# First mixture of a two-layer kernel: seven masked products of weight differences and one unmasked product per slot, router bias on TensorE, beta rows added during the scan, new orders

## The chip, the cores and the metric

The kernel runs on one core of a Trainium2 chip. The metric is the device time of one execution in microseconds, as the median of several runs. Engines are named as in the profile: PE is TensorE, DVE VectorE, ACT ScalarE, POOL GpSimd, SP SyncE, whose queue issues most DMAs.

## The reference, cut to what matters

Two layers over x of 16 x 512 tokens and 128 channels. Each has an attention-like half and a mixture of experts with adaLN modulation. The change touches the first layer: its state-space scan, and its mixture, in which each token goes through the one expert with the highest logit.

```python
h = _layernorm(x) * (1 + ca) + sa
x = x + ga * _L0_attn_ref(h, ...)       # scan over 512 tokens, then y = (y - mu) * rsqrt(var + eps) * gamma + beta
h = _layernorm(x) * (1 + cb) + sb
x = x + gb * _L0_ffn_ref(h, ...)

# _L0_ffn_ref, 8 experts:
logits = xt @ gate_w + gate_b
sel = jnp.argmax(softmax(logits), axis=-1)
onehot = one_hot(sel, 8)
y_all = einsum('td,edh->eth', xt, expert_w) + expert_b[:, None, :]
out = einsum('te,eth->th', onehot, y_all)
```

## The kernel before, in words

The program is a row of stages, each a block in which every engine has its own hand-written instruction list; the lists meet only through semaphores. A stage ends at a barrier of all engines (`end_phase`). Each engine runs its list strictly in order, so the order of the calls in a list is the schedule.

The tokens are cut into 16 slots `w` of 512 tokens (`C` = 4 tiles of 128). `x_tok` holds x with tokens on partitions, `xg` the scan's result.

**The scan** (block before `ssm.close()`). 16 groups of 8 channels pass through a pipeline, one step per group. PE multiplies the group into end states (L687), carries them over (L695) and writes outputs (L705 with `carry`, L709 with Toeplitz tiles `toep`). DVE masks (L646), adds (L652), reduces (L656) and spreads the end states into `carry` in three copies (L665), each a product of `ends` and a piece of `con`, both in SBUF. ACT stores the outputs (L634). SP loads twelve Toeplitz tiles (L623), each after the output product four groups before. POOL clears `carry` (L675) and then waits for the barrier.

**The first mixture** (block from `names = ("weights", ...`). For each slot:

- DVE: `statistics` (L1006, L1010) of the scan's result; `gamma` (L1034 for the first four slots, L1039 behind them); `joined` (L1049, L1053) adds to `x_tok`; `stats_x` and `shift_x_head` (L1017 to L1026) for the first four slots.
- POOL: `beta` (L883) adds the row ga * beta to `x_tok` before `joined`; `bias_pieces` (L888 to L899) cuts the experts' biases into three bf16 parts, with a one-time wait on six weight loads; the means and scales of the normalizations (L843 to L866).
- ACT: roots, normalizations, `feat` (L966), which writes the modulated and transposed features `f_t`; `hot_half` (L973); `scaled` (L979), which takes the finished product; squares (L924).
- PE: `turn` (L1124) transposes the normalized tiles, `logits` (L1132), `turn_hot` (L1140) transposes the one-hot choices, `bias` (L1156) starts the sum in PSUM, then eight products (L1160), one per expert, `ew0[:, e, :]` times `masked[e % 4]`, and `turn_back` (L1148).
- DVE: `best` (L1060 to L1072) adds the router's bias to the logits, takes the largest and the first that equals it, and writes the one-hot choices `hot`. `mask` (L1090), eight per slot, multiplies `f_t` by one expert's row of ones and zeros, spread over the partitions (`wide`). `added` (L1081) adds the product.
- SP: `load` (L800) fetches the rows ga * gamma and ga * beta of a slot; `kept` (L817) writes the choices to DRAM and `spread` (L822) reads them back broadcast to 128 partitions.

The eight masks share four buffers. So a mask waits for the product four before it, and a product for its mask:

```python
def mask(w, e):
    if e == 0:
        landed(dve, s_wide, w)
        done(dve, "feat", w)
    expert(dve, "product", w, e - 4)
    nc.vector.tensor_tensor(masked[e % 4][:, :], f_t[w % W][:, :], wide[w % W][:, e, :], ALU.mult)

def product(w, e):
    expert(pe, "masked", w, e)
    nc.tensor.matmul(ps[:, w % 2, :], ew0[:, e, :], masked[e % 4][:, :], start=False, stop=(e == E - 1))
```

`idle_products` (L69) are products of the identity that nobody reads; they stand where PE would wait.

## Time and profile before

| what | us |
|---|---|
| median of 3 runs (lowest, highest) | 947.99 (942.74, 949.33) |
| the profiled execution | 940.09 |
| its span, first to last instruction | 938.3 |
| PE, DVE, ACT, POOL busy in the span | 863.5, 773.4, 627.1, 566.3 |
| mean granted TensorE clock, share of full speed | 0.983 |
| scan, in us of the span | 98.5 to 142 |
| first mixture, in us of the span | 143.0 to 339.1 |

Busy times in rows of several instructions are of their union; a duration in the timeline runs from the first start to the last end. A matmul in fp32 stands as two records, and its end is modelled, so a product's pace is read from starts. Brackets behind an instruction give how long its engine had been idle and what ended that.

### The profile page before, as it was taken

The page shows a single profiled execution, that of the slowest core. Times are in us where ns is not written, and L with a number is a line of the kernel's source. Part 1 is how long each engine was busy: PE and PEld are TensorE (multiplying, and loading weights), DVE is VectorE, ACT ScalarE, POOL GpSimd, SP SyncE. Part 2 cuts the span into 40 slices and gives each one's busy share as a digit, 9 for nine tenths or more (in the row PEclk, how much of TensorE's full clock was granted, in tenths as well). Part 3 has the DMA queues.
Part 4 walks back from the last instruction along what each step waited for, and adds up shares of the span by engine and source line. Part 5 has one row for each costly group of instructions (what it writes and reads, how often), then busy time and mean ns, then how long its engine had stood idle before and what let it go on. Part 6 is the DMA issues. An engine that isn't in the chain of part 4 may idle for free.

```text
span 938.3 us, 24334 instructions
## 1 busy us (share of the span) xinstructions
PE 863.5 (92%) x7820; PEld 682.3 (73%) x7820; DVE 773.4 (82%) x2369; ACT 627.1 (67%) x1619; POOL 566.3 (60%) x551
## 2 busy tenths in 40 slices
PE   6979897898999979999999999999979999999990
PEld 5945677544454468888888888888758888888880
DVE  3988778999999736888999999999996866666996
ACT  3557123578788355567777777766567888888880
POOL 1211004397776215433888888888877777777773
PEclk9999998999999999999999999999999999999996
DMA  5330352333322212000011111111127765766987
GB/s 156 95 96 1 99 174 64 113 136 111 139 96 91 100 30 56 2 1 10 31 41 40 39 36 36 39 37 45 41 63 229 213 201 180 224 183 201 345 254 248
DMA packets 83465, 100.84 MB, mean 107 GB/s; under 512 B 15326, under 2 KB 65305, under 8 KB 81164
## 3 DMA queue, kind: packets, MB, share of 16 engines
q1 hardware_dynamic: 71388, 79.61, 27.7%
q0 software_dynamic: 8640, 17.97, 5.4%
q10 hardware_dynamic: 3312, 1.70, 0.6%
q8 instruction: 65, 1.06, 0.5%
q14 instruction: 60, 0.49, 0.2%
HBM read 75.71 MB, written 23.54 MB: 106 GB/s over the span
## 4 chain that ended last, share of the span: by engine, by line
PE 54%; DVE 3%; ACT 2%; issue 2%; DMA 1%; POOL 1%; SPq 0%; ACTq 0%; DVEq 0%; POOLq 0%
PE ps L2697 12%; PE ps L2435 12%; PE ps L2720 6%; PE ps L2451 4%; PE ps L2513 2%; PE ps L2426 2%; PE ps L2446 2%; PE ps L2680 2%; PE ps L2552 2%; PE ps L2568 2%; PE ps L2414 1%; PE ps L2401 1%; PE ps L2500 1%; POOL parts L1651 1%; PE ps L69 1%
## 5 line engine op out<-in xcount | busy, mean ns | idle before, releaser
L1618 POOL TENSOR_TENSOR kvb<-qk,v 128x1024 f32<-128x1024 f32 x64 | 127.1, 1990 | 71.7 <-DVE qk L1991 48.0
L1627 POOL DMA_INDIRECT rows_of<-payb,posu x128 | 143.8, 1124 | 39.5 <-issue 28.4
L2435 PE MATMUL ps<-con,kvb 128*128 128x128 f32 x1024 | 126.0, 276 | 0.0
L1160 PE MATMUL ps<-masked,ew 128*128 128x512 f32 x256 | 121.3, 603 | 2.3 <-DVE masked L1090 2.3
L2435 PEld LDWEIGHTS ps<-con,kvb 128*128 128x128 f32 x1024 | 119.4, 192 | 1.0 <-issue 1.0
L2362 DVE TENSOR_SCALAR qk<-ps,b 128x256 f32<-128x256 f32 x142 | 62.0, 478 | 46.8 <-PE ps L2697 41.6
L1651 POOL DMA_INDIRECT parts<-h,dest x72 | 79.6, 1106 | 23.6 <-issue 20.3
L1090 DVE TENSOR_TENSOR masked<-f_t,wide 128x512 f32<-128x512 f32 x128 | 86.9, 724 | 4.7 <-PE ps L1160 4.5
L1651 POOL DMA_INDIRECT parts<-gx,dest x70 | 77.8, 1111 | 21.4 <-issue 19.5
L1967 DVE TENSOR_TENSOR qc<-ps,qk 128x1024 f32<-128x1024 f32 x64 | 78.0, 1219 | 11.8 <-PE ps L2435 10.8
L1160 PEld LDWEIGHTS ps<-masked,ew 128*128 128x128 f32 x256 | 44.3, 190 | 43.9 <-issue 29.3
L2720 PE MATMUL ps<-w,f_t 128*128 x568 | 75.0, 275 | 0.0
L2720 PEld LDWEIGHTS ps<-w,f_t 128*128 128x128 f32 x568 | 69.0, 192 | 8.2
L1872 ACT ACTIVATE qk<-ps,b 128x256 f32<-128x256 f32 x142 | 59.6, 470 | 17.3 <-PE ps L2697 16.7
L2697 PE MATMUL ps<-qd,ex 128*128 128x256 f32 x288 | 68.1, 379 | 0.0
L2697 PE MATMUL ps<-qd,lg 128*128 128x256 f32 x280 | 66.3, 380 | 0.0
L69 PE MATMUL ps<-con 128*128 128x128 f32 x398 | 55.7, 294 | 4.9 <-PEq L74 3.9
L69 PEld LDWEIGHTS ps<-con 128*128 128x128 f32 x398 | 51.6, 207 | 8.1 <-issue 6.7
L2697 PEld LDWEIGHTS ps<-qd,ex 128*128 128x128 f32 x288 | 51.9, 190 | 5.6
L1877 ACT ACTIVATE nrm<-qk,limit 128x512 f32<-128x512 f32 x71 | 51.3, 722 | 6.8
L2251 DVE SCALAR_TENSOR_TENSOR f_t<-qk,nrm 128x512 f32<-128x512 f32 x71 | 49.2, 694 | 7.1 <-DVE qk L2362 0.8
L2697 PEld LDWEIGHTS ps<-qd,lg 128*128 128x128 f32 x280 | 50.5, 190 | 5.4
(375 smaller groups left out, 2142.4 us busy)
## 6 DMA issues: line engine op xcount, KB each, us to landing
wide<-hot_dram SPq DMA_DIRECT2D x16, 1024.0 KB, 4.6
kvb<-rows_of SPq DMA_DIRECT2D x71, 132.0 KB
ex<-in_w_dram SPq DMA_DIRECT2D x36, 256.0 KB
lg<-in_w_dram SPq DMA_DIRECT2D x35, 256.0 KB
toep<-taps_dram SPq DMA_DIRECT2D x16, 512.0 KB, 4.4
xg<-parts SPq DMA_DIRECT2D x16, 512.0 KB, 5.5
x_tok<-in_x_dram SPq DMA_DIRECT2D x16, 256.0 KB, 3.0
rows<-rows_dram SPq DMA_DIRECT2D x16, 192.0 KB, 3.1
```

What stands on the lines that cost most here:

```text
L69: nc.tensor.matmul(ps[:, bank, 0:P], k("ident"), k("ident"), start=True, stop=True)
L1090: nc.vector.tensor_tensor(masked[e % 4][:, :], f_t[w % W][:, :], wide[w % W][:, e, :], ALU.mult).then_inc(s["masked"], 1)
L1160: nc.tensor.matmul(ps[:, w % 2, :], ew0[:, e, :], masked[e % 4][:, :], start=False, stop=(e == E - 1)).then_inc(s["product"], 1)
L1618: nc.gpsimd.tensor_tensor(kv[g % KB][:, :, :].rearrange("p e (h d) -> p e h d", h=H), k_in, v_in, ALU.mult).then_inc(s["kv"], 1)
L1627: nc.gpsimd.indirect_dma_start(rows_of, bass.IndirectOffsetOnAxis(ap=posu[w % PR][:, slot, t:t + 1], axis=0), pay[w % PB][:, t, :], None). ...
L1651: nc.gpsimd.indirect_dma_start(parts, bass.IndirectOffsetOnAxis(ap=dest[:, at, c:c + 1], axis=0), yw[u][:, c, :], None).then_inc(s_out[u], 16)
L1872: last = nc.scalar.activation(glu[v % 2][:, f, :], ps[:, bank, f * SP:(f + 1) * SP], ACT.Relu, bias=b1[:, bass.ds(e * NF + f, 1)], scale=-1.0)
L1967: nc.vector.tensor_tensor(qc[g % 2][:, :, :], cum(g), q_in, ALU.mult).then_inc(s["qc"], 1)
L2362: last = nc.vector.tensor_scalar(lin[v % 2][:, f, :], ps[:, bank + 1, f * SP:(f + 1) * SP], b1[:, bass.ds(e * NF + 2 + f, 1)], 8.0, ALU.ad ...
L2435: last = nc.tensor.matmul(cum(g)[:, e, :], kv[g % KB][:, e, :], k("upto"), start=True, stop=True)
L2697: last = nc.tensor.matmul(ps[:, bank + f // 2, (f % 2) * SP:(f % 2 + 1) * SP], w1c[v % WC][:, f * P:(f + 1) * P], x_t[v % 2][:, :], start= ...
L2720: last = nc.tensor.matmul(to, act_t[v % 2][:, j, c * P:(c + 1) * P], w2[:, bass.ds(e * (2 * D) + j * D, D)], start=False, stop=(c == S - 1 ...
```

## The change

- The weights `ew0[e]` of experts 0 to 6 become differences to those of expert 7 (one POOL subtraction). A slot's sum is now an unmasked product of `f_t` with `ew0[7]` (`base`) and seven masked ones (`M` = 7); `base` starts the sum in PSUM, `bias` comes behind it. The four masked buffers go round over all masks, not per slot.
- The router's bias, divided by 8 and cut into three bf16 parts on 24 rows (`gb3`), is added on PE by a product with a tile of ones at the start of `logits`; `best` reads the logits from PSUM (two readers) and has no addition.
- The additions of the beta rows leave the mixture. SP loads all 16 rows, broadcast to 128 partitions (`betas`, 1 MB), and the weights at the start of the scan; POOL does the preparations and 16 additions to `x_tok` beside the scan. `rows` hold the gamma rows alone.
- The lists of POOL, ACT, DVE, SP and PE in the mixture have a new order; PE has fewer idle products.

```diff
+                    sp.dma_start(ebf[0:E, :], a["eb0"]).then_inc(s_ahead, 16)
+                    sp.dma_start(ebf[E:2 * E, :], a["eb0"]).then_inc(s_ahead, 16)
+                    sp.dma_start(ebf[2 * E:K3, :], a["eb0"]).then_inc(s_ahead, 16)
+                    sp.dma_start(gbf[:, :], a["gb0"].partition_broadcast(K3)).then_inc(s_ahead, 16)
+                    sp.dma_start(gw0[:, :], a["gw0"]).then_inc(s_ahead, 16)
+                    sp.dma_start(ew0[:, :, :], a["ew0"]).then_inc(s_ahead, 16)
+                    sp.dma_start(betas[:, :, :], rows_dram[:, D:2 * D].partition_broadcast(P)).then_inc(s_ahead, 16)
                     groups(sp, body)
...
                     for u in range(U):
                         nc.gpsimd.memset(carry[u][:, :, :], 0.0).then_inc(s_z, 1)
...
+                    pool.wait_ge(s_ahead, 7 * 16)
+                    pool.wait_ge(s_split, 3)
+                    nc.gpsimd.tensor_tensor(ew0[:, 0:M, :], ew0[:, 0:M, :], ew0[:, M:E, :].to_broadcast([P, M, D]), ALU.subtract).then_inc(s_ew, 1)
+                    pieces(s_split, ebf, ebh, ebr, 3, [which[:, j:j + 1] for j in range(2)])
...
+                    for b in range(B):
+                        at = x_tok[:, b * C:(b + 1) * C, :]
+                        nc.gpsimd.tensor_tensor(at, at, betas[:, b:b + 1, :].to_broadcast([P, C, D]), ALU.add).then_inc(s_beta, 1)
...
                         if e == 0:
                             landed(dve, s_wide, w)
                             done(dve, "feat", w)
-                        expert(dve, "product", w, e - 4)
-                        nc.vector.tensor_tensor(masked[e % 4][:, :], f_t[w % W][:, :], wide[w % W][:, e, :], ALU.mult).then_inc(s["masked"], 1)
...
+                        at = w * M + e
+                        if at >= 4:
+                            expert_product(dve, (at - 4) // M, (at - 4) % M)
+                        nc.vector.tensor_tensor(masked[at % 4][:, :], f_t[w % W][:, :], wide[w % W][:, e, :], ALU.mult).then_inc(s["masked"], 1)
...
-                            done(pe, "lg", w - 1)
+                            done(pe, "equal", w - 1)
+                            nc.tensor.matmul(ps[:, LOGIT, 0:C * E], one3[:, :], gb3[:, :, :].rearrange("p c e -> p (c e)"), start=True, stop=False)
                             done(pe, "feat", w)
...
+                    def base(w):
+                        done(pe, "moe_t", w - 2)
+                        done(pe, "feat", w)
+                        nc.tensor.matmul(ps[:, w % 2, :], ew0[:, M, :], f_t[w % W][:, :], start=True, stop=False).then_inc(s["plain"], 1)
...
-                    statistics(0); statistics(1); gamma(0); joined(0); stats_x(0); gamma(1); shift_x_head(0); joined(1); stats_x(1)
+                    statistics(0); gamma(0); joined(0); stats_x(0); statistics(1); shift_x_head(0); gamma(1); joined(1); stats_x(1)
```

On POOL, the mixture's list began like this before; L883 are the beta additions, L888 to L899 the bias pieces:

```order
L901 MEMSET eps 128x1
L902 TENSOR_SCALAR down<-con 128x8
L883 TENSOR_TENSOR x_tok<-x_tok,rows_73 128x512
L883 TENSOR_TENSOR x_tok<-x_tok,rows_74 128x512
L888 TENSOR_SCALAR which<-con 24x1 x2
L890 TENSOR_SCALAR which<-which 24x2
L893 CAST ebh<-ebf 24x128
L895 TENSOR_SCALAR ebr<-ebh,which 24x128
```

Now the scan's list of POOL ends like this, behind the subtraction of the experts' weights (L724) and the pieces of both biases; `betas` are the rows, L638 is the branch out of the scan's block:

```order
L711 CAST gbh<-gbf 24x8
L713 TENSOR_SCALAR gbr<-gbh,which 24x8
L715 TENSOR_TENSOR gbf<-gbf,gbr 24x8
L730 CAST gb_13<-gbf 24x32
L733 TENSOR_TENSOR x_tok<-x_tok,betas 128x512 x16
L638 UNCONDITIONAL_BRANCH
```

All sixteen additions moved in front of the barrier, and they stand in one run.

On DVE, the masks of slot 0 and the choice of slot 2 stood like this before:

```order
L1090 TENSOR_TENSOR masked_108<-f_t_92,wide_100 128x512
L1060 TENSOR_TENSOR logit<-ps,gb_72 128x32
L1063 TENSOR_REDUCE largest<-logit 128x4
L1065 TENSOR_TENSOR equal<-logit,largest 128x32
L1067 TENSOR_TENSOR equal<-equal,down 128x32
L1069 TENSOR_REDUCE lowest<-equal 128x4
L1072 TENSOR_TENSOR hot<-down,lowest 128x96
L1090 TENSOR_TENSOR masked_109<-f_t_92,wide_100 128x512
L1090 TENSOR_TENSOR masked_106<-f_t_93,wide_101 128x512
```

The same place now (`masked_114` is slot 0's last mask, `f_t_99` belongs to slot 1):

```order
L1106 TENSOR_TENSOR masked_114<-f_t_98,wide_106 128x512
L1043 SCALAR_TENSOR_TENSOR stat_89<-moments_x,stat_88 128x4
L1077 TENSOR_REDUCE largest<-ps 128x4
L1079 TENSOR_TENSOR equal<-ps,largest 128x32
L1081 TENSOR_TENSOR equal<-equal,down 128x32
L1083 TENSOR_REDUCE lowest<-equal 128x4
L1086 TENSOR_TENSOR hot<-down,lowest 128x96
L1106 TENSOR_TENSOR masked_115<-f_t_99,wide_107 128x512
```

The eighth mask and the addition to the logits are gone, and a shift of the head (L1043) stands behind the first masks.

On PE, the change from slot 6 to slot 7 before (L1132 logits of slot 9, L1156 the bias, L1140 the choices, L1148 the turn back):

```order
L1132 MATMUL ps<-gw_71,f_t_93 128x8 x4
L1156 MATMUL ps<-hot_b_99,ebx 128x512
L1160 MATMUL ps<-masked_106,ew_65 128x512
L1160 MATMUL ps<-masked_107,ew_65 128x512
L1140 MATMUL ps<-con,hot 24x128 x4
L1148 MATMUL ps<-con,moe_t_104 128x128 x4
```

and now, at the same slots (L1168 `base`, L1172 the bias, L1143 the ones times the router's bias, L1162 the turn back):

```order
L1176 MATMUL ps<-masked_112,ew_5 128x512
L1137 MATMUL ps<-con,xn_97 128x128 x4
L1168 MATMUL ps<-f_t_101,ew_5 128x512
L1172 MATMUL ps<-hot_b_105,ebx 128x512
L1143 MATMUL ps<-gb_13,one_14 128x32
L1146 MATMUL ps<-gw_18,f_t_99 128x8 x4
L1176 MATMUL ps<-masked_113,ew_5 128x512
L1162 MATMUL ps<-con,moe_t_110 128x128 x4
```

A product that waits for no mask stands at the slot's change, in the place of the eighth masked one.

## Rows read from the trace of the kernel before

**Rows 1.** Windows: stretch, then busy us (count) of PE, PEld, DVE, ACT, POOL.
```profile
98.50:142.00 43.50, 40.51 (x768) 28.09 (x768) 32.86 (x113) 9.55 (x16) 1.92 (x4) 1.00 0.51 147
...
143.00:173.40 30.40, 24.84 (x176) 22.70 (x176) 29.11 (x121) 13.30 (x34) 13.99 (x20) 0.89 0.31 96
173.40:309.50 136.10, 128.95 (x480) 64.97 (x480) 130.77 (x484) 106.65 (x331) 95.01 (x153) 1.00 0.31 111
309.50:331.70 22.20, 22.20 (x65) 10.06 (x64) 16.27 (x45) 6.91 (x27) 7.99 (x12) 1.00 0.23 86
```

**Rows 2.** Timeline of PE, one slot: start, us, engine, line, what.
```profile
236.88 0.66 PE L1148 MATMUL ps<-con,moe_t 128*128 128x128 f32 x4
...
239.53 3.60 PE L1160 MATMUL ps<-masked,ew 128*128 128x512 f32 x8
242.97 0.60 PE L1124 MATMUL ps<-con,xn 128*128 128x128 f32 x4
...
246.04 0.38 PE L1156 MATMUL ps<-hot_b,ebx 24*128 24x512 bf16 x1
246.36 1.13 PE L1160 MATMUL ps<-masked,ew 128*128 128x512 f32 x2
```

**Rows 3.** Timeline of PE at the end, and line L1160 in all (first and last start).
```profile
316.42 1.98 PE L1160 MATMUL ps<-masked,ew 128*128 128x512 f32 x4
...
324.24 1.13 PE L1160 MATMUL ps<-masked,ew 128*128 128x512 f32 x2
...
L1160 PE MATMUL ps<-masked,ew x256: 592/592/697, 174.1 to 331.2; 128*128 128x512 f32 x128
```

**Rows 4.** Timeline of the scan, PE and DVE, one step.
```profile
110.97 1.06 PE L705 MATMUL ps<-carry,states_of 128*64 128x512 f32 x4
...
112.01 0.98 DVE L665 TENSOR_TENSOR carry<-ends,con 128x128 f32<-128x128 f32 x3
...
113.42 1.06 PE L705 MATMUL ps<-carry,states_of 128*64 128x512 f32 x4
113.44 0.42 DVE L646 TENSOR_TENSOR endm<-ps,odd 128x256 f32<-128x256 f32 x1 [0.44 <-PE ps L687]
```

**Rows 5.** Groups by line, DVE from 173.4 to 309.5: busy us, mean ns, idle before.
```profile
L1090 DVE TENSOR_TENSOR masked<-f_t,wide 128x512 f32<-128x512 f32 x108 | 73.2, 730 | 1.5 <-PE ps L1160 1.5
...
L1060 DVE TENSOR_TENSOR logit<-ps,gb 128x32 f32<-128x32 f32 x14 | 2.5, 176 | 0.6 <-PE ps L1132 0.6
```

**Rows 6.** Timeline of DVE and POOL about 205, and line L1090 (ns, min/median/max).
```profile
204.97 2.36 DVE L1090 TENSOR_TENSOR masked<-f_t,wide 128x512 f32<-128x512 f32 x2
...
205.06 1.72 POOL L883 TENSOR_TENSOR x_tok<-x_tok,rows 128x512 f32<-128x512 f32 x1
206.75 0.67 POOL L843 TENSOR_SCALAR stat<-stat 128x4 f32<-128x4 f32 x1
...
L1090 DVE TENSOR_TENSOR masked<-f_t,wide x128: 658/682/1757, 173.4 to 328.4; 128x512 f32<-128x512 f32 x128
```

**Rows 7.** Timeline of the mixture's head, DVE and POOL.
```profile
145.94 2.55 POOL L883 TENSOR_TENSOR x_tok<-x_tok,rows 128x512 f32<-128x512 f32 x2 [2.58 <-DMA rows<-rows_dram]
...
146.60 2.74 DVE L1034 SCALAR_TENSOR_TENSOR yn<-xg,moments,rows 128x128 f32<-128x128 f32 x4
...
155.07 4.93 POOL L883 TENSOR_TENSOR x_tok<-x_tok,rows 128x512 f32<-128x512 f32 x4
...
157.66 2.36 DVE L1026 SCALAR_TENSOR_TENSOR stat<-moments_x,stat 128x4 f32<-128x4 f32 x1
...
159.95 1.45 DVE L1034 SCALAR_TENSOR_TENSOR yn<-xg,moments,rows 128x128 f32<-128x128 f32 x4
```

**Rows 8.** DMAs: the Toeplitz loads' timeline and time to landing; the page's broadcast load.
```profile
105.63 12.64 SPq L623 DMA_DIRECT2D toep<-taps_dram  x6
...
DMA to landing us min/median/max: 3.7/4.3/5.6
...
wide<-hot_dram SPq DMA_DIRECT2D x16, 1024.0 KB, 4.6
```

More of the change, by code:

```diff
@@ new lines, in _ @@
+                    pieces(s_split, ebf, ebh, ebr, 3, [which[:, j:j + 1] for j in range(2)])
+                    nc.gpsimd.tensor_copy(ebx[:, :], ebf[:, :]).then_inc(s_split, 1)
+                    nc.gpsimd.tensor_scalar(gbf[:, :], gbf[:, :], 1.0 / E, None, ALU.mult).then_inc(s_split, 1)
+                    pool.wait_ge(s_split, 11)
+                    pieces(s_split, gbf, gbh, gbr, 11, [which[:, j:j + 1] for j in range(2)])
+                    nc.gpsimd.tensor_copy(gb3[:, :, :], gbf[:, :].unsqueeze(1).to_broadcast([K3, C, E])).then_inc(s_split, 1)
@@ L810, in load_ahead @@
                             done(sp, "gamma", w)
-                            done(sp, "beta", w)
                             load(w + W)
@@ L1043, in joined @@
                             done(dve, "gamma", w)
-                            done(dve, "beta", w)
                             if w < HEAD:
@@ L1214, in _ @@
-                    product(15, 2); product(15, 3); product(15, 4); product(15, 5); product(15, 6); product(15, 7)
+                    idle_products(FREE, 4)
+                    product(0, 0); product(0, 1); product(0, 2); product(0, 3); product(0, 4); product(0, 5); product(0, 6); product(1, 0)
+                    turn_back(0); turn_hot(2); product(1, 1); product(1, 2); product(1, 3); turn(3); product(1, 4); product(1, 5); logits(3)
+                    product(1, 6); base(2); bias(2); turn_hot(3); turn_back(1); base(3); product(2, 0); product(2, 1); turn(4)
@@ new lines, in _ @@
+                    product(2, 2); product(2, 3); product(2, 4); logits(4); product(2, 5); product(2, 6); bias(3); turn_hot(4)
+                    product(3, 0); product(3, 1); product(3, 2); turn(5); turn_back(2); product(3, 3); product(3, 4); logits(5)
+                    product(3, 5); product(3, 6); base(4); turn_hot(5); turn(6); bias(4); turn_back(3); product(4, 0); product(4, 1)
+                    logits(6); product(4, 2); product(4, 3); product(4, 4); turn(7); turn_hot(6); product(4, 5); product(4, 6); logits(7)
@@ new lines, in _ @@
+                    base(5); bias(5); turn_back(4); turn_hot(7); product(5, 0); product(5, 1); product(5, 2); product(5, 3); product(5, 4)
+                    turn(8); product(5, 5); product(5, 6); base(6); logits(8); bias(6); turn_back(5); product(6, 0); product(6, 1)
+                    turn_hot(8); product(6, 2); product(6, 3); product(6, 4); product(6, 5); product(6, 6); turn(9); base(7); bias(7)
+                    logits(9); product(7, 0); turn_back(6); product(7, 1); product(7, 2); turn_hot(9); product(7, 3); product(7, 4)
@@ new lines, in _ @@
+                    turn(10); product(7, 5); product(7, 6); logits(10); base(8); bias(8); product(8, 0); turn_hot(10); turn_back(7)
+                    product(8, 1); product(8, 2); product(8, 3); product(8, 4); product(8, 5); turn(11); product(8, 6); base(9); logits(11)
+                    bias(9); turn_back(8); product(9, 0); product(9, 1); turn_hot(11); product(9, 2); product(9, 3); product(9, 4); turn(12)
+                    product(9, 5); product(9, 6); base(10); logits(12); bias(10); turn_back(9); product(10, 0); product(10, 1); turn_hot(12)
@@ new lines, in _ @@
+                    product(10, 2); product(10, 3); product(10, 4); turn(13); product(10, 5); product(10, 6); logits(13); base(11)
+                    turn_back(10); bias(11); turn_hot(13); product(11, 0); product(11, 1); product(11, 2); product(11, 3); product(11, 4)
+                    turn(14); product(11, 5); product(11, 6); logits(14); base(12); turn_back(11); bias(12); turn_hot(14); product(12, 0)
+                    product(12, 1); product(12, 2); product(12, 3); product(12, 4); turn(15); product(12, 5); product(12, 6); logits(15)
```

268 lines of the change are left out of this document (114 added, 154 removed).

## The prediction

> **What bounds the kernel now.** I read the windows by stage first. The mixture stage of the first layer runs from 143.0 to 339.1 us of the profiled span. In its first 30.4 us DVE is busy 29.1. From the first masked copy at 173.4 to 309.5, DVE is busy 130.8 of 136.1 us and PE 129.0. From 309.5 to 331.7 PE never stops while DVE is busy 16.3 of 22.2 [rows 1]. DVE sets the pace until 309.5, PE at the end, and PE is close behind all the way.
>
> How close, the timeline of PE tells. From 236.88 to 246.36 it does one of everything that a slot needs (one turn back, one turn, one turn of the choices, logits, bias, eight products): 9.48 us, of which some 0.06 is waiting, so 9.42 [rows 2]. At the end, without turn, logits and choices, a slot is 324.24 - 316.42 = 7.82 us [rows 3]. After the first product PE has 13 slots of the first kind and 3 of the second: 13 x 9.42 + 3 x 7.82 = 146 us. The products run from 174.1 to 331.2 plus the last one's 0.4 [rows 3], so 157.5 us: PE loses 11 to 12 us in all. That is the most this stage can give after its head, whatever DVE is relieved of.
>
> The scan before it (98.5 to 142, DVE busy 32.9 of 43.5 [rows 1]) repeats one step per group of channels. PE starts the same product at 110.97 and 113.42: 2.45 us a step. DVE's carry copies end at 112.01 + 0.98 = 112.99, 0.43 us before PE's product with them at 113.42; and DVE is idle 0.44 us a step [rows 4]. POOL does nothing there.
>
> **The change, part by part.** Sums are against the profiled execution, 940.09 us with a span of 938.3; the three timed runs have a median of 947.99, so I add the difference to that.
>
> *Masks and logits on DVE.* One of eight masks per slot goes. 108 of them keep DVE busy 73.2 us [rows 5]; without the port waits below (5.2 us) that is 0.63 each, so 16 x 0.63 = 10 us. The bias addition to the logits goes, 0.18 us each [rows 5] plus a gap, 14 x 0.22 = 3 us after the head. Its two readers now read PSUM; the addition did so at no visible price, so I cost that at nothing.
>
> *Beta rows off POOL in this stage.* The pair of masks at 204.97 takes 2.36 us, where a pair alone is 1.26; POOL's addition that begins across it at 205.06 takes 1.72 us instead of 1.23, and POOL's tiny next instruction, at 206.75, takes 0.67 [rows 6]. They take turns, one whole instruction each. How many masks are hit: their mean is 730 ns [rows 5], their median 682 [rows 6], and 108 x 0.048 = 5.2 us, five masks of up to 1757 ns. That comes back to DVE. The Trainium skill, "SBUF — State Buffer", section on ports, says that a DVE instruction with two SBUF inputs and a GpSimd instruction that reads SBUF exclude each other for a whole instruction; the trace agrees, by these rows.
>
> DVE's need after the head is then 130.8 + 16.3 - 10 - 3 - 5.2 = 128.9 us, some 133 with gaps. That is under PE's 146, so PE becomes the bound.
>
> *PE.* Seven masked products and one unmasked (base) are eight products still: no gain. New is one bf16 product of 32 columns per logits, 13 after the head; the trace has no such form. Its ends are nothing and the bias product's 0.32 us (246.04 to 246.36 [rows 2]); I take 0.1, 1.3 us in all. base(0) and base(1) are done before the first product, and that takes 2 x 0.86 = 1.7 us away (four products from 239.53 to 242.97 give 0.86 each [rows 2]). PE's floor stays near 145.5. PE reached 92% of its floor's pace while DVE was full; with DVE at 90% I take 96.5%, 151 us, a gain of 7 (bounds 0 and 12).
>
> *The head.* POOL's two additions at 145.94 stretch DVE's four operations at 146.60 to 2.74 us, where the same four take 1.45 at 159.95: 1.3 us. The four additions from 155.07 hold one tiny DVE operation of 157.66 for 2.36 us instead of 0.2: 2.1 us. Two logit additions, the wait for POOL's `down` and a shift moved behind the masks: 1.0 us. Against it, gamma(0) now stands ahead of statistics(1), and its rows land only at 145.94, 1.2 us after DVE is ready for them. Sum 3.2; I take 3 (bounds 1 and 5) [rows 7]. The weights that were awaited on PE and POOL are there already; PE's path there was hidden by DVE.
>
> So the stage gives 3 + 7 = 10 us.
>
> *The scan receives.* SP issues seven loads ahead of its twelve Toeplitz loads, the last one 1 MB of beta rows in 512-byte pieces, like the Toeplitz ones: 512 KB of those take 4.3 us to land, so 1 MB takes 4.6 (another 1 MB form) to 8.6 and lands at 106 to 111. The first Toeplitz load goes out at 105.63, as the first out product of 1.1 us ends, and its buffer is read again four steps after that product began: 105.6 - 1.1 + 9.8 = 114.3. It lands near 109.9, so it has 4.4 us of cover [rows 8]. I cost the queue at nothing; it would be up to 4 us if that cover went.
>
> POOL then has one subtraction of 896 columns, some fifteen tiny operations and sixteen beta additions, with no wait between the sixteen. Each one reads two SBUF tensors, and DVE's three carry copies a step read two SBUF tensors as well. That is the pair which excluded each other above. The trace has no POOL work beside the scan, so I bound it. If the carry copies slip through: 0. If they win at each end of an addition, as the masks did, a step becomes three additions and three short copies, 3 x (1.23 + 0.25) = 4.4 us instead of 2.45. The 1.23 is 4.93 / 4 of the run at 155.07 [rows 7]; the 0.25 lies below a copy's third of 0.98 [rows 4]. Sixteen additions last 5.3 steps: 5.3 x 1.95 = 10.4 us. If DVE loses at each end, as the operation of 157.66 did (it sat through the end at 158.8), the scan stands still: 16 x 1.23 = 19.7 us. I take the middle case. The masks of rows 6 won at every such end; and of DVE's four operations at 146.60 (1.45 us alone, over at 149.34) some must have run before POOL's pair ended at 148.49, so one got in between two additions. The subtraction is 2.2 us by 1.23 for 512 columns, less the 0.43 of slack: 0 to 1.7, taken 1.2. The tiny ones can cost no more than what the slack leaves of each: taken 0.4. Sum 12 us. POOL's tiny instructions of before fit, waits included, between 148.49 and 155.07 [rows 7], 6.6 us at most, and the router's are as many: POOL ends by 111 + 2 + 13 + 23 = 149, before a scan that would end at 154, so it adds nothing of its own.
>
> By the rule of that page of the Trainium skill alone the scan's loss would be one of the last two cases, never the first; no run here shows the carry copies beside POOL.
>
> **Sum.** -10 + 12 = +2 us: 942 in a profiled execution, 950 on the scale of the median.
>
> **The rivals.**
> 1. *The beta run starves the scan (slower).* Place: DVE L665 (L694 now) beside POOL L733. Price 19.7 + 1.6 = 21.3 us, less 10: +11, so 959. For it: the operation of 157.66 did sit through the end of an addition at 158.8, and here sixteen stand without a wait. Against it: between the additions from 145.94 one got in. It decides when fewer than three steps pass during the run.
> 2. *The scan hardly notices.* +1 us, and the stage gives 10 to 14: -11, so 937. For it: the carry's inputs are 16 and 8 numbers per partition, repeated, and no row shows such a form beside POOL; if the loads land late, part of the run falls beside the drain of the scan. Against it: rows 6 and 7.
> 3. *The stage reaches PE's floor, and the scan loses only 6 to 8.* 12 + 5 gained, 7 lost: -10, so 938. For it: DVE's slack of 12 us, base and bias that cover the wait of the turn back. Against it: only four masked buffers, 3.4 us of PE's work.
> 4. *The new orders don't get it.* The unmasked product and longer chains leave new waits on PE, the stage gives 3: +9, so 957. For it: DVE's other work stands in bursts between the masks, and PE waited at them before too. Against it: the load on DVE falls by 18 us.
>
> **Chances.** Forecast (+2, own range -5 to +9) 0.42; rival 1 0.18; rival 2 0.22; rival 3 0.10; rival 4 0.08. A difference of 1%, 9.5 us, is about what a measurement of this kernel can tell. Of the forecast 0.01 is faster by that and 0.07 slower; of rival 1 0.12 slower; of rival 2 0.15 faster; of rival 3 0.08 faster; of rival 4 0.07 slower. That makes 0.24 faster, 0.26 slower, 0.50 the same. The range goes from rival 2 and a little (935) to just past rival 1 (962).
>
> **What would show it.** Right, if in the new profile the scan's span grows from 43.5 to about 55 us, with carry copies over 1 us beside L733, and the mixture's span falls from 196 to about 186 with PE busy over 96% from the first product on. The head: first masked copy some 30 - 3 us after the stage's start. Wrong, if the scan keeps its 2.45 us step while POOL adds (then rival 2), if it stands still for a stretch of many additions (rival 1), or if PE's idle time before products with DVE as the releaser stays at its size (rival 4).

## The result, and the profile after

Twenty runs of the changed kernel have a median of 951.7 us (949.67 to 954.79), twenty of the kernel before 943.9 (938.0 to 953.22). The ratio is 1.0082, with an interval of 1.0064 to 1.0101: the change costs 7.8 us. The profiled execution's span is 950.2 us, 11.9 over the span before; the execution profiled before lay below the median of its kernel, so the spans show more than the medians do.

The forecast was 950.0, and 951.7 lies in its range and within 1% of the kernel before. Of the sum's two large terms the stage's was right and the scan's was not.

The windows by stage, of the changed kernel: scan, mixture up to the first masked copy, first masked copy to last product, what is left (stretch, its length, then busy us and count of PE, PEld, DVE, ACT, POOL, the granted clock, the share of the DMA engines, GB/s).

```profile
98.50:165.00 66.50, 43.47 (x768) 30.10 (x768) 53.98 (x113) 9.55 (x16) 29.83 (x42) 0.85 0.41 120
166.10:192.90 26.80, 19.97 (x129) 16.41 (x129) 24.57 (x118) 13.20 (x34) 0.00 (x0) 0.94 0.20 66
192.90:343.00 150.10, 149.20 (x551) 75.82 (x552) 131.71 (x500) 112.88 (x358) 87.56 (x156) 1.00 0.30 110
343.00:350.40 7.40, 4.62 (x39) 4.23 (x37) 0.92 (x8) 2.34 (x9) 1.66 (x4) 0.98 0.01 2
```

These answer to [rows 1]. The mixture is what the prediction wanted it to be. From the first masked copy to the last product PE is busy 149.2 of 150.1 us, and DVE only 131.7: the bound has gone from DVE to PE. The scan, 43.5 us long before, takes 66.5. DVE's busy time there rose from 32.9 to 54.0 with the same 113 instructions, so one of them must be very long. The granted clock is 0.85 where it was 1.00.

The timeline of DVE and POOL in the scan of the changed kernel shows which one (start, length, engine, line, operation, count, and in brackets the idle time ahead and what ended it):

```profile
107.10 2.82 DVE L694 TENSOR_TENSOR carry<-ends,con 128x128 f32<-128x128 f32 x3
107.56 2.12 POOL L724 TENSOR_TENSOR ew<-ew 128x896 f32<-128x896 f32 x1 [5.77 <-DMA betas<-rows_dram]
...
113.50 1.01 DVE L694 TENSOR_TENSOR carry<-ends,con 128x128 f32<-128x128 f32 x3
...
115.96 20.29 DVE L694 TENSOR_TENSOR carry<-ends,con 128x128 f32<-128x128 f32 x3
115.97 19.54 POOL L733 TENSOR_TENSOR x_tok<-x_tok,betas 128x512 f32<-128x512 f32 x16
```

DVE's group of three carry copies, 1.01 us at 113.50, takes 20.29 at 115.96. POOL's run of sixteen additions begins 0.01 us later and lasts 19.54. The line's own statistics (ns: min/median/max), first of the kernel before, then of the changed one, show that a single copy holds nearly all of it:

```profile
L665 DVE TENSOR_TENSOR carry<-ends,con x48: 375/390/418, 102.6 to 138.2; 128x128 f32<-128x128 f32 x48
```
```profile
L694 DVE TENSOR_TENSOR carry<-ends,con x48: 366/396/19795, 102.6 to 161.4; 128x128 f32<-128x128 f32 x48
...
L733 POOL TENSOR_TENSOR x_tok<-x_tok,betas x16: 1249/1250/1264, 116.0 to 134.3; 128x512 f32<-128x512 f32 x16
```

One copy of 0.4 us took 19.8 us. It is the first of its group, as the same line shows when only what runs between 116.1 and 135.5 is asked for:

```profile
L694 DVE TENSOR_TENSOR carry<-ends,con x1: 19795/19795/19795, 116.0 to 116.0; 128x128 f32<-128x128 f32 x1
```

Its record opens at 115.96, 0.01 us before that of the first addition, but the reduction ahead of it on DVE (L685, from 115.44) lasts 0.60 us, to 116.04; by then the addition ran. The copy waited through all fifteen boundaries between additions and ended at 135.75, when the sixteenth was over; the other two of its group took 0.37 us each behind it. POOL, on its side, never waited: its sixteen additions differ by 15 ns.

How the scan's 23 us come together can be counted on PE, which starts the same output product once a step, 2.45 us apart in the kernel before [rows 4]. The timeline of PE in the changed kernel:

```profile
106.06 1.06 PE L763 MATMUL ps<-carry,states_of 128*64 128x512 f32 x4
...
109.97 1.08 PE L763 MATMUL ps<-carry,states_of 128*64 128x512 f32 x4 [1.30 <-DVE carry L694]
...
112.45 1.06 PE L763 MATMUL ps<-carry,states_of 128*64 128x512 f32 x4
...
114.91 1.06 PE L763 MATMUL ps<-carry,states_of 128*64 128x512 f32 x4
...
136.35 1.98 PE L763 MATMUL ps<-carry,states_of 128*64 128x512 f32 x4 [18.82 <-issue]
...
143.90 1.07 PE L763 MATMUL ps<-carry,states_of 128*64 128x512 f32 x4
```

From 106.06 to 109.97 are 3.91 us, 1.5 over a step of 2.45 us: that is POOL's subtraction at 107.56. From 114.91 to 136.35 are 21.44, 19.0 over: the run of additions. From 136.35 to 143.90 are two steps in 7.55 us, 2.6 over, and no POOL work stands beside them. There PE itself is slow: the product that takes 1.06 us takes 1.98 at 136.35, just after PE had been idle for 18.8 us. The granted clock is 0.50, the lower level of 1.2 GHz, from 136.2 to 141.3, and 1.00 again from 143.9. 1.5 + 19.0 + 2.6 = 23.1 us.

The masks of the changed kernel, against [rows 6]:

```profile
L1106 DVE TENSOR_TENSOR masked<-f_t,wide x112: 658/684/707, 192.9 to 339.8; 128x512 f32<-128x512 f32 x112
its engine sat idle before it (us, times) until:
  PE ps L1176: 7.6, 26
```

Their maximum is 707 ns, where it was 1757: no mask waits for POOL any more. Now DVE waits for PE before masks, 7.6 us in 26 places, and the groups by line have PE waiting only 1.2 us for them:

```profile
L1176 PE MATMUL ps<-masked,ew 128*128 128x512 f32 x224 | 103.1, 596 | 1.2 <-DVE masked L1106 1.2
```

The whole account, in one measure. For each kernel of this study the trace gives four stretches: the scan, from POOL's first clearing of `carry` to the end of the last carry copy; the drain, to the mixture's first statistics; the head, to the first product with a masked tile; and the products, to the end of the last one, taken as 0.4 us behind its start (the label is the experiment's below; us). The last column is not in one measure: the runs of e1 to e4, of e5 to e8, and of e9 and e10 were timed in three rounds, each beside runs of the kernel before, whose medians were 944.4, 945.8 and 944.1. The ratios given below are to those.

| kernel | scan | drain | head | products | median of the runs |
|---|---|---|---|---|---|
| before | 40.1 | 4.7 | 30.7 | 157.5 | 943.9 |
| after | 63.2 | 4.4 | 27.4 | 149.5 | 951.7 |
| e1 | 40.1 | 4.4 | 27.5 | 149.5 | 930.41 |
| e2 | 46.9 | 4.4 | 27.9 | 149.4 | 936.82 |
| e3 | 42.3 | 9.0 | 27.5 | 149.5 | 937.4 |
| e4 | 41.4 | 4.7 | 27.9 | 153.6 | 933.34 |
| e5 | 61.9 | 4.4 | 28.0 | 151.9 | 955.4 |
| e6 | 40.9 | 4.9 | 27.5 | 153.6 | 935.42 |
| e7 | 41.5 | 4.4 | 31.8 | 154.8 | 942.36 |
| e8 | 42.5 | 4.4 | 28.0 | 149.4 | 931.18 |
| e9 | 43.7 | 4.3 | 27.5 | 149.5 | 932.4 |
| e10 | 41.6 | 4.6 | 28.1 | 152.0 | 936.52 |

The scan of the kernel before took 40.1 us in one execution and 41.4 in another (before and e4, whose scans are the same code); the whole difference stands in one early step, and its cause is open. POOL's subtraction costs another 0 to 1.5 us, by where in a step it falls. So less than 2.4 us is not read from the scan's column; where it matters below, single steps are compared. After against before: scan +23.1, drain -0.3, head -3.3, products -8.0; with 0.4 from all that follows, +11.9 in the spans.

### The profile page after: what moved, and what is told of

Read it like the earlier page. It is cut to its first block and busy times, and to the rows that moved or that the text cites. A ratio compares the mean times of both kernels' runs of the same rounds, so it can differ in the third digit from the quotient of the medians.

```text
span 950.2 us, 24163 instructions
## 1 busy us (share of the span) xinstructions
PE 858.4 (90%) x7758; PEld 679.6 (72%) x7774; DVE 778.1 (82%) x2337; ACT 626.0 (66%) x1619; POOL 563.2 (59%) x561
## 3 DMA queue, kind: packets, MB, share of 16 engines
q1 hardware_dynamic: 73344, 79.60, 27.4%
## 5 line engine op out<-in xcount | busy, mean ns | idle before, releaser
L1634 POOL DMA_INDIRECT rows_of<-payb,posu x128 | 143.9, 1125 | 39.5 <-issue 27.6
L1176 PE MATMUL ps<-masked,ew 128*128 128x512 f32 x224 | 103.1, 596 | 1.2 <-DVE masked L1106 1.2
L1106 DVE TENSOR_TENSOR masked<-f_t,wide 128x512 f32<-128x512 f32 x112 | 72.8, 685 | 8.3 <-PE ps L1176 7.6
L1176 PEld LDWEIGHTS ps<-masked,ew 128*128 128x128 f32 x224 | 39.6, 190 | 38.7 <-issue 32.1
L69 PE MATMUL ps<-con 128*128 128x128 f32 x336 | 48.7, 298 | 7.7 <-PEq L74 4.7
L69 PEld LDWEIGHTS ps<-con 128*128 128x128 f32 x336 | 45.0, 210 | 11.7 <-issue 8.2
```

Source lines behind the costliest of these rows:

```text
L69: nc.tensor.matmul(ps[:, bank, 0:P], k("ident"), k("ident"), start=True, stop=True)
L1106: nc.vector.tensor_tensor(masked[at % 4][:, :], f_t[w % W][:, :], wide[w % W][:, e, :], ALU.mult).then_inc(s["masked"], 1)
L1176: nc.tensor.matmul(ps[:, w % 2, :], ew0[:, e, :], masked[(w * M + e) % 4][:, :], start=False, stop=(e == M - 1)).then_inc(s["product"], 1)
L1634: nc.gpsimd.indirect_dma_start(rows_of, bass.IndirectOffsetOnAxis(ap=posu[w % PR][:, slot, t:t + 1], axis=0), pay[w % PB][:, t, :], None). ...
```

## The experiments

The theory was: the additions alone make the scan longer, by keeping DVE's carry copies from an SBUF port over the whole run; everything else in the change gains. Its rivals: the seven new loads or the subtraction do part of the damage, POOL's instructions as such (not their reads) disturb DVE, and the gain in the mixture comes from the masks and not from the additions that left.

**e1: the changed kernel without its additions.**

```diff
-                    for b in range(B):
-                        at = x_tok[:, b * C:(b + 1) * C, :]
-                        nc.gpsimd.tensor_tensor(at, at, betas[:, b:b + 1, :].to_broadcast([P, C, D]), ALU.add).then_inc(s_beta, 1)
```

> The changed kernel without its sixteen beta additions on POOL; the output lacks the row ga * beta, all loads and the other preparations stay. If the run of additions holds the shared port through (my rival 1), the carry copy of 19.8 us beside it falls to 0.4, and with it the slow step behind it (PE at the lower clock): 20 to 21.5 us less than the changed kernel, about 931 against 951.7 in the median, ratio to the kernel before about 0.987. If the copy waited for something else that falls in the same stretch (the 1 MB load, a semaphore), the long copy stays and at most 2 us are gained.

Measured: 930.41 us, ratio 0.9848 (0.9791 to 0.9905). The scan is 40.1 us, that of the kernel before to a tenth, with the loads, the subtraction and the cutting of the biases still in it. So the loads and their queue cost nothing, and here the subtraction, which began at another point of a step, stretched one group of copies to 1.23 us and cost nothing either. The additions, with the slow steps of PE behind them, are the whole of the loss but for the 1.5 us that the subtraction took in the changed kernel.

**e8: sixteen fillings of memory in place of the additions.** As many elements each, written into a tile of their own, reading nothing.

```diff
+            blank = sb("blank", [P, B, C, D], scope=sc)
...
-                        at = x_tok[:, b * C:(b + 1) * C, :]
-                        nc.gpsimd.tensor_tensor(at, at, betas[:, b:b + 1, :].to_broadcast([P, C, D]), ALU.add).then_inc(s_beta, 1)
+                        nc.gpsimd.memset(blank[:, b, :, :], 0.0).then_inc(s_beta, 1)
```

> The changed kernel with each beta addition replaced by a POOL memset of 512 columns to a tile of its own (about 0.48 us each, some 7.7 us in one run without a gap); the output lacks the row ga * beta. If what excludes DVE is the read of SBUF by POOL (the rule of the Trainium skill), no carry copy is held: all last 0.4 us and the scan is as long as before. If any busy POOL holds the port, one copy lasts about 7 us and the scan is 6 us longer.

Measured in one run: 931.18 us. The timeline of POOL and of DVE beside it:

```profile
115.56 7.51 POOL L733 MEMSET blank<- 128x512 f32 x16
```
```profile
115.87 1.04 DVE L695 TENSOR_TENSOR carry<-ends,con 128x128 f32<-128x128 f32 x3
...
118.34 1.02 DVE L695 TENSOR_TENSOR carry<-ends,con 128x128 f32<-128x128 f32 x3
...
120.79 1.01 DVE L695 TENSOR_TENSOR carry<-ends,con 128x128 f32<-128x128 f32 x3
```

POOL runs sixteen instructions without a gap for 7.5 us, and three groups of copies pass beside it in 1.0 us each, as ever. The scan of 42.5 us has 1.3 us in an early step and 1.1 at the subtraction, and nothing beside the fillings. So a busy POOL is not what stops DVE; what the fillings lack, the reading of SBUF, is. The page "SBUF — State Buffer" of the Trainium skill (section "SBUF: two separate sides") has DVE instructions with two SBUF inputs excluded only by GpSimd instructions that read SBUF, and this case agrees.

**e2: a gap between the additions.** Each addition waits for the semaphore of the one before it, which POOL would have kept the order of anyway.

```diff
                     for b in range(B):
+                        if b:
+                            pool.wait_ge(s_beta, b)
```

> The changed kernel with one more wait on POOL before each addition, for the addition before it, so that no two stand back to back. If only a run without a gap shuts DVE out, DVE gets in at each end: a step lasts three additions and three short copies, 4.4 us, sixteen additions cost the scan 10.4 us instead of 19.3, so 8 to 10 us less than the changed kernel, about 943. If POOL keeps the port over the gap, or always wins, nothing changes: 951 to 952.

Measured: 936.82 us, ratio 0.9899 (0.9843 to 0.9955), 15 us less than the changed kernel for one wait. The timeline of POOL, the additions among the groups (busy us, mean ns, idle before), the timeline of DVE and line L694 from the first addition on (ns):

```profile
119.66 23.13 POOL L735 TENSOR_TENSOR x_tok<-x_tok,betas 128x512 f32<-128x512 f32 x16
```
```profile
L735 POOL TENSOR_TENSOR x_tok<-x_tok,betas 128x512 f32<-128x512 f32 x16 | 22.0, 1372 | 1.2
```
```profile
123.58 2.04 DVE L694 TENSOR_TENSOR carry<-ends,con 128x128 f32<-128x128 f32 x3
...
126.49 2.02 DVE L694 TENSOR_TENSOR carry<-ends,con 128x128 f32<-128x128 f32 x3
...
L694 DVE TENSOR_TENSOR carry<-ends,con x33: 386/427/1406, 120.0 to 148.2; 128x128 f32<-128x128 f32 x33
```

The additions' group has 1.2 us of idle time in all, so a gap is 1.2 / 15 = 0.08 us, and some additions are now held by a copy (the mean is 1372 ns, where each took 1250). That is enough: no copy beside the additions lasts longer than 1.41 us, that is, none waits for more than one addition. It goes better than the turn-taking of the prediction. A step takes 2.9 us (123.58 to 126.49), which is two additions with their gaps, and not the 4.4 us of three: two of the three copies pass at one gap and the third at the next. The scan is 6.8 us longer than that of e1, of which 4.4 belong to the additions (46.9 against 42.5 in e8, which has the same early step and about the same loss at the subtraction), where the prediction's middle case had 10.4.

**e3: one addition a step.** Addition `b` waits for DVE's own count of spread groups.

```diff
+                        pool.wait_ge(s2['spread'], min(b + 6, G))
```

> The changed kernel with each addition waiting for one more carry spread of the scan (at least b + 6, at most 16). Each begins when DVE has just released its copies, and lasts 1.25 us, while DVE asks for the port again 1.48 us later. By the port theory ten additions cost nothing and the last six follow the scan's last copies and hold the barrier: 6 x 1.25 less the drain of 2 us, some 5 us. So about 14 us less than the changed kernel and the scan some 8 us longer than before: near 937, ratio about 0.993. If the additions slow the scan otherwise than by the port, steps with one addition grow over 2.6 us and the gain is under 8.

Measured: 937.4 us, ratio 0.9915 (0.9886 to 0.9943). The timeline:

```profile
118.97 1.28 POOL L734 TENSOR_TENSOR x_tok<-x_tok,betas 128x512 f32<-128x512 f32 x1 [1.20 <-DVE carry L694]
...
140.41 7.38 POOL L734 TENSOR_TENSOR x_tok<-x_tok,betas 128x512 f32<-128x512 f32 x6 [0.85 <-DVE carry L694]
```
```profile
149.33 1.20 DVE L1024 BATCH_NORM_STATS2 halves<-xg 128x6 f32<-128x128 f32 x4 [9.00 <-PEq L74]
```

An addition that begins when the copies of its step are done is over (1.28 us) before those of the next begin (1.45 later), and costs nothing. But only ten fit. The last six come in a run after the last copy and hold the barrier: the drain is 9.0 us instead of 4.4. The theory's number was met.

**e4: the kernel before without its additions in the mixture,** each replaced by the filling of one element.

```diff
-                            nc.gpsimd.tensor_tensor(tiles(x_tok, w), tiles(x_tok, w), rows[w % W][:, 1:2, :].to_broadcast([P, C, D]), ALU.add).then_inc(s["beta"], 1)
+                            nc.gpsimd.memset(junk_b[:, w:w + 1], 0.0).then_inc(s["beta"], 1)
```

> The kernel before with its sixteen beta additions replaced by tiny memsets (the output lacks the row ga * beta). It shows what the port cost the old mixture. By the theory DVE gets back 3.4 us in the head and 5.2 in the middle; the head's are on the path at once, of the middle's the most, since DVE is full there and PE can give 12: 6 to 9 us less than the kernel before, first masked copy at 170. If PE was the real bound of the middle, only the head's 3.4 come.

Measured: 933.34 us, ratio 0.9867 (0.9812 to 0.9922). With all eight masks, the logit additions and the old orders in place, the head is 2.8 us shorter and the products 3.9: 6.7 us for the sixteen additions' leaving.

**e7: the changed kernel with its additions in the mixture again.** New masks, new logits, new orders, and `beta(w)` about where it was in POOL's list. Not quite: before, the bias pieces (L888 to L899) stood between the second addition and the third, and here they are in the scan, so that the first four additions stand in a row.

```diff
-                    for b in range(B):
-                        at = x_tok[:, b * C:(b + 1) * C, :]
-                        nc.gpsimd.tensor_tensor(at, at, betas[:, b:b + 1, :].to_broadcast([P, C, D]), ALU.add).then_inc(s_beta, 1)
...
+                    beta(0); beta(1); beta(2); beta(3); beta(4); beta(5); beta(6); beta(7)
```

> The changed kernel with all sixteen additions in the mixture's POOL list, where the kernel before had them, and nothing but the weights' preparations in the scan. Scan as before; the head loses again what the additions beside it cost, 3 to 4 us, the middle 0 to 4. So mixture 188 to 192 us against 184.3, in all 936 +- 3, ratio about 0.992: slower than the paced version by 3 to 7 us. If it ties with the paced version, moving any of the additions was worth nothing.

Measured: 942.36 us, ratio 0.997 (0.9939 to 1.0001). A miss: 6 us more than expected. The head is 31.8 us, 1.1 more than before, and the products 154.8, 2.7 less. So with the additions left in the mixture the masks, the logits and the orders gain 1.6 us. Without any additions they gain 4.5 (e1 against e4: head 0.4, products 4.1). The additions' leaving gains 6.7 in the old mixture (e4) and 9.6 in the new one (e1 against e7: head 4.3, products 5.3). Both together are 11.2 either way, so 2.9 us depend on what the other part does.

Half of the 2.9 lies in the head, and the trace of e7 shows where. The first four additions run beside DVE's first four `gamma` operations, which take 0.42 us each where nothing is beside them (1.45 for the four, [rows 7]). The timeline of POOL, and the line of `gamma` from 146.0 to 151.5:

```profile
146.63 5.07 POOL L930 TENSOR_TENSOR x_tok<-x_tok,rows 128x512 f32<-128x512 f32 x4 [35.37 <-DMA rows<-rows_dram]
```
```profile
L1061 DVE SCALAR_TENSOR_TENSOR yn<-xg,moments,rows x4: 1347/1348/1372, 146.7 to 150.5; 128x128 f32<-128x128 f32 x4
```

Each operation waits for one addition: the group takes 5.19 us, against 2.74 beside the pair of [rows 7] and 1.44 in e1. Of the 4.3 us that the additions cost this head, 3.7 are these. So the 1.6 us understates the masks, the logits and the orders, by a new place of the first additions that the change itself does not have. In the products a mask still takes up to 1757 ns,

```profile
L1117 DVE TENSOR_TENSOR masked<-f_t,wide x112: 657/684/1757, 174.4 to 326.9; 128x512 f32<-128x512 f32 x112
```

and why the additions cost 5.3 us there and 3.9 before was not taken apart.

**e5: the eighth mask put back,** as a product into a tile that nobody reads, one per slot.

```diff
+                        if e == 3:
+                            nc.vector.tensor_tensor(spare[w % 2][:, :], f_t[w % W][:, :], wide[w % W][:, M, :], ALU.mult).then_inc(s["spare"], 1)
```

> The changed kernel with one more masked copy per slot on DVE, into a tile nobody reads (0.63 us each, 10 us in all); the result is unchanged. It tells whether DVE or PE bounds the new mixture. With PE as the bound (149.5 us of products against a floor of 145.5, DVE's need 129) most of the ten fits into DVE's slack: the products' stretch grows by 1 to 4 us. If DVE still bounds it, by 8 to 10.

Measured: 955.4 us, ratio 1.0094 (1.006 to 1.0127). The products take 151.9 us against 149.5. The window of the products' stretch in e5, and the masks among DVE's groups in the changed kernel from 192.9 to 320.0:

```profile
191.70:344.70 153.00, 151.50 (x563) 76.43 (x563) 139.67 (x515) 112.92 (x358) 90.02 (x156) 1.00 0.30 109
```
```profile
L1106 DVE TENSOR_TENSOR masked<-f_t,wide 128x512 f32<-128x512 f32 x95 | 61.0, 684 | 5.2 <-PE ps L1176 4.6 <-issue 0.2
```

DVE is busy 139.7 us there instead of 131.7, the stretch grows by 2.4, and where the masks are, DVE had been idle 5.2 us in the changed kernel, 4.6 of it for PE. Of the 8.0 us of added work 2.4 show, under a third: DVE has slack, and PE bounds the stretch.

**e6: nine additions a step apart in the scan, seven in the mixture** (slots 9 to 15), so that none is left for the drain.

```diff
-                    for b in range(B):
+                    pool.wait_ge(s_landed, 16)
+                    for b in range(9):
+                        pool.wait_ge(s2["spread"], b + 5)
...
+            LATE = 9
```

> A version meant to beat both: nine beta additions in the scan, each behind one more carry spread (at least b + 5), the other seven in the mixture's list of POOL for slots 9 to 15, their rows loaded with the gamma rows as before. By the port theory the nine cost nothing, since each starts as DVE has released its copies; the seven hit a mask each at 1.1 us at most, and DVE now has slack. Scan as before (last carry copy at 138.7 from a start at 98.5), mixture 184 to 187 us, in all 19 to 22 us less than the changed kernel: 930 to 933, ratio 0.986 to 0.989.

Measured: 935.42 us, ratio 0.9886 (0.9846 to 0.9926). It beats both kernels, but by 2 to 5 us less than expected. The scan does as was thought (40.9), and the products take 153.6, 4.1 more than in e1. The seven late additions, each with a mask or another DVE operation behind it, cost 0.6 us apiece.

**e10: twelve in the scan, four in the mixture,** to see whether that price goes by the piece.

```diff
-                    for b in range(9):
+                    for b in range(12):
...
-            LATE = 9
+            LATE = 12
```

> As the kernel with nine additions in the scan and seven in the mixture, with twelve in the scan (behind steps 5 to 16) and four in the mixture (slots 12 to 15). If each late addition costs the products 4/7 us, the stretch is 153.6 - 1.7 = 151.9 us and the scan's end moves by 0 to 1 us: 934 to 935. If only the early ones of the seven late additions cost (they stand where PE has its longest slots), the stretch is back to 150 us: 932. If the number doesn't matter, 153.6 stays: 936.

Measured: 936.52 us, ratio 0.9911 (0.9878 to 0.9944). The products take 152.0 us, where 151.9 was asked for by the first of the three readings: 0.6 us for each late addition. The time is nevertheless not below that of e6. Of the 1.6 us that the products gained, the scan's end takes back 0.7: its last two groups of copies, beside the eleventh and the twelfth addition, take 1.68 and 1.74 us,

```profile
139.38 1.68 DVE L695 TENSOR_TENSOR carry<-ends,con 128x128 f32<-128x128 f32 x3
141.43 1.74 DVE L695 TENSOR_TENSOR carry<-ends,con 128x128 f32<-128x128 f32 x3
```

where those of e6 take 1.00. The head is 0.6 longer in this execution, for which no cause was looked for, and the two intervals overlap widely.

**e9: all sixteen in the scan,** three steps with two of them, each with a gap, and the last two after the last copy.

```diff
-                    pool.wait_ge(s_ahead, 7 * 16)
+                    pool.wait_ge(s_ahead, 6 * 16)
...
+                    pool.wait_ge(s_landed, 16)
+                    due = (5, 6, 7, 7, 8, 9, 9, 10, 11, 11, 12, 13, 14, 15, 16, 16)
                     for b in range(B):
+                        pool.wait_ge(s2["spread"], due[b])
+                        if b:
+                            pool.wait_ge(s_beta, b)
```

> The changed kernel with all sixteen additions in the scan, each behind a step of DVE's spreading (5, 6, 7, 7, 8, 9, 9, 10, 11, 11, 12, 13, 14, 15, 16, 16) and behind the end of the addition before it, and the beta rows awaited only after the subtraction. Theory A (a pair of additions in one step costs that step 0.4 to 0.5 us, one addition costs nothing, and the late additions alone cost the kernel with nine and seven its 4 us of products): three pairs cost the scan 1.5, the last two additions hold the barrier by 0 to 2 us, the products' stretch is back to 149 to 150 us; 3 us below the kernel with nine and seven, so 931 to 934. Theory B (the products' stretch was longer there for another cause than the additions): it stays at 153 us or more, and the time is 935 to 938.

Measured: 932.4 us (930.59 to 933.31, six runs), ratio 0.987 (0.9838 to 0.9902): the lowest median of the kernels that compute everything. Its slowest run is below the fastest of e10, timed in the same round (933.31 and 933.86 us); from e6 it is not told apart by the ratios' intervals. The timeline, POOL and then DVE:

```profile
119.72 2.86 POOL L739 TENSOR_TENSOR x_tok<-x_tok,betas 128x512 f32<-128x512 f32 x2 [1.17 <-DVE carry L695]
123.12 1.28 POOL L739 TENSOR_TENSOR x_tok<-x_tok,betas 128x512 f32<-128x512 f32 x1 [0.55 <-DVE carry L695]
...
143.09 2.69 POOL L739 TENSOR_TENSOR x_tok<-x_tok,betas 128x512 f32<-128x512 f32 x2 [0.85 <-DVE carry L695]
```
```profile
118.64 1.00 DVE L695 TENSOR_TENSOR carry<-ends,con 128x128 f32<-128x128 f32 x3
...
121.10 1.94 DVE L695 TENSOR_TENSOR carry<-ends,con 128x128 f32<-128x128 f32 x3
...
123.96 1.22 DVE L695 TENSOR_TENSOR carry<-ends,con 128x128 f32<-128x128 f32 x3
...
126.66 1.94 DVE L695 TENSOR_TENSOR carry<-ends,con 128x128 f32<-128x128 f32 x3
...
147.32 1.21 DVE L1029 BATCH_NORM_STATS2 halves<-xg 128x6 f32<-128x128 f32 x4 [4.32 <-PEq L74]
```

A pair of additions stretches the copies of the next step to 1.94 us, and the single addition behind it those of the step after to 1.22: the two steps from 121.10 to 126.66 take 5.56 us instead of 4.91, so a pair costs 0.65. The last two are over at 145.78, within the 4.3 us of the drain, and hold nothing. The products are back at 149.5, as theory A had it. The scan is 3.6 us over the shortest: 1.9 for the three pairs, 0.9 at the subtraction, and 0.7 at the end, where the steps are shorter than 2.45 us and the last two groups take 1.65 and 1.74 us.

## Why the prediction was right, and where it was wrong

**The bound and the stage: right.** DVE's need after the head was put at 128.9 us, and the window shows 131.7 busy; PE was to become the bound, and it is (e5). The head was to give 3 us and gave 3.3 to 3.7, by whether one counts from the first statistics or from the stage's first operation. The products' stretch was to fall to 151 us and fell to 149.5: 8 gained where 7 were taken. The masks' stretches to 1757 ns are gone, as the port waits of [rows 6] asked. The router's extra product costs what it was priced at: 0.12 us from its start to the next, 0.1 taken.

**What the stage's gain rests on: only half seen.** The prediction charged 10 us of DVE to the masks, 3 to the logits and 5.2 to the port, and let PE's floor cut the sum. In that reading the first two would have done most of it alone. The runs show 4.5 us for them without the additions, 1.6 with them (e7, whose first four additions cost the head more than before), and 6.7 us for the additions alone (e4). The port waits stand as stretches of 1 us and more at single masks, and PE, with four masked buffers, seems to feel a late mask more than an average load; no run changed the number of buffers.

**The scan: the term that failed.** The step reads: "If they win at each end of an addition, as the masks did, a step becomes three additions and three short copies ... I take the middle case." The middle case was 10.4 us. The runs show the case that stood beside it with 19.7: the copy loses at every one of fifteen ends (19.0 us by PE's starts), which was rival 1, given 0.18. The middle case itself was also mis-sized: where it came true, in e2, a step took 2.9 us and not 4.4.

The rows were read rightly, and carried too far. The trace of the kernel before does show DVE getting in between two additions: the first two of the four `gamma` operations beside the pair of [rows 7], asked for one at a time,

```profile
146.60 0.77 DVE L1034 SCALAR_TENSOR_TENSOR yn<-xg,moments,rows 128x128 f32<-128x128 f32 x1
...
147.30 1.35 DVE L1034 SCALAR_TENSOR_TENSOR yn<-xg,moments,rows 128x128 f32<-128x128 f32 x1
```
```profile
145.94 1.27 POOL L883 TENSOR_TENSOR x_tok<-x_tok,rows 128x512 f32<-128x512 f32 x1 [2.58 <-DMA rows<-rows_dram]
...
147.17 1.32 POOL L883 TENSOR_TENSOR x_tok<-x_tok,rows 128x512 f32<-128x512 f32 x1
```

are over at 147.37 and 148.65, each just behind one addition, and in e7 DVE gets in at all three boundaries of a run of four. What differs in the source is that each addition of the mixture stands behind a wait for its rows (`landed(pool, s_rows, w)`), and the sixteen of the scan behind none. The prediction names this under rival 1 ("here sixteen stand without a wait") and gives it no weight in the sum. e2 puts a wait in front of each of them, and DVE gets in. A wait is not all there is to it: the tiny operation of 157.66 sat through the boundary of 158.75 between two additions that have such waits. No run kept everything else and changed only the waits in the mixture, so what decides there stays open.

**A term that was missing.** The stall leaves PE idle for 18.8 us, and the two steps behind it run partly at the lower clock: 2.6 us. The starved case was therefore undercounted too: 21.3 us were forecast for it, 23.1 came.

**The small terms.** The subtraction was taken at 1.2 us and cost 1.5 in the changed kernel, 1.1 in e8, 0.9 in e9 and nothing in e1: it depends on where in a step it starts. The beta rows landed by 107.56, at the early end of 106 to 111, and neither they nor the Toeplitz loads behind them made anything wait, since e1 with all seven loads has the scan of the kernel before.

**Why the sum still came out.** By the spans it was -10 + 12 = +2 forecast and -11.3 + 23.1 = +11.9 (with the drain and the rest) measured: 10 us off. By the medians the kernel lies 7.8 above the one before. The forecast of 950.0 was added to a median of three runs, 947.99, that twenty runs put at 943.9. That 4 us offset is luck, and it hid 4 of the 6 us by which the difference itself was wrong (+2 forecast, +7.8 measured). The other 4 us between the spans (+11.9) and the medians (+7.8) are that the execution profiled before, 940.09, was a fast one of its kernel. So the time came out within 2 us with a scan that was 11 us off.

## What to carry to other kernels

Work that is moved to an idle engine is not free when it keeps an engine on the critical loop from SBUF: look for two-input DVE operations beside POOL operations that read SBUF, and above all for POOL instructions that stand back to back with no wait between them, since their whole run can count as one wait. Pace them with a semaphore that the critical engine already counts, one for each step where the step's gap holds it (e3: no cost for ten; e9: 951.7 to 932.4 us with all sixteen, at 0.65 us for each pair that shares a step). When a change has several parts that relieve one engine, undo each by itself and also leave each alone, since what one gains depends on the other (1.6 or 4.5 us here); and check that the part put back stands where it stood.

## What the runs showed of the hardware that was not expected

A run of back-to-back POOL additions with no wait between them kept DVE out at fifteen of fifteen boundaries: one copy of 0.4 us stretched to 19.8. e5, which has the same run, shows the same group of copies at 20.29 us. The page "SBUF — State Buffer" of the Trainium skill (section "SBUF: two separate sides") speaks of an exclusive lock held for the whole instruction, by whichever starts first. The trace agrees for one instruction, and shows more than the sentence says for a run of them: DVE, waiting, was not served in between.

With a wait in front of each addition DVE was served: in e2, where the wait is for the addition before and leaves a gap of 0.08 us, and in e7, where the waits were met before (the rows had landed at 147.03, 148.18 and 148.51, for additions that began at 147.85, 149.12 and 150.39) and POOL's additions began no more than 1.27 us apart, against 1.22 in the run without waits. The operations that waited were not the same ones, copies in one and `gamma` in the other. How the port is handed over between two instructions, the traces do not tell.

After 18.8 us of idleness PE's product took 1.98 us and the next but one 1.07, as before the stall, with a granted clock of 0.50 until 141.3. So a stall on the loop costs more than its length, here by 14%.
